# FFN1 of a layer-norm, attention and 8-bit FFN kernel: w1's blocks are turned before their trip through DRAM instead of after it

## The reference, cut to what matters

```python
def _ste_quant_rows(a):
    scale = jnp.maximum(jnp.max(jnp.abs(a), axis=-1, keepdims=True) / 127.0, 1e-08)
    return jnp.clip(jnp.round(a / scale), -127.0, 127.0) * scale

def _linear8bit(x, W, b):
    col_max = jnp.max(jnp.abs(x), axis=tuple(range(x.ndim - 1)))
    outlier = col_max > 3.0
    x_in, x_out = jnp.where(outlier, 0.0, x), jnp.where(outlier, x, 0.0)
    return _ste_quant_rows(x_in) @ _ste_quant_rows(W).T + x_out @ W.T + b

xn = _layernorm(x)                                  # x: (4, 512, 512) float32
s = attention(xn, wq, wk, wv, wo)                   # causal, 32 heads of 16, one k and v head
h = _linear8bit(xn, W1, b1)                         # W1: (2048, 512)   <- FFN1
g = silu(_linear8bit(h, W2, b2))                    # W2: (512, 2048)   <- FFN2
out = x + s * g
```

## Time and profile before

| | before |
|---|---|
| time, median of 3 runs | 804.09 us (801.3 to 804.69) |
| profiled execution, its time | 802.13 us |
| span of its instructions | 800.4 us |
| mean granted clock of TensorE | 0.981 of full speed |
| TensorE matmul busy | 756.8 us, 95% |
| TensorE weight load busy | 569.1 us, 71% |
| VectorE busy | 650.9 us, 81% |
| ScalarE busy | 395.4 us, 49% |
| GpSimd busy | 274.5 us, 34% |
| DMA packets under 512 B, of all | 71808 of 115276 |

### The profile page before, as it was taken

One profiled execution on the slowest core, in us unless ns is written; L12 is line 12 of the kernel. 1 busy time (PEld: TensorE's weight loads), 2 busy tenths in 40 slices (PEclk: granted clock), 3 DMA queues, 4 the chain that ended last, 5 costly groups with the idle time before them and its releaser, 6 DMA issues. The chain is left out here.

```text
span 800.4 us, 11979 instructions
## 1 busy us (share of the span) xinstructions
PE 756.8 (95%) x4133; PEld 569.1 (71%) x4133; DVE 650.9 (81%) x1115; ACT 395.4 (49%) x670; POOL 274.5 (34%) x349
## 2 busy tenths in 40 slices
PE   5999999999999999999998998899997999999995
PEld 4878665556776767766576876688886788888884
DVE  7988999999999899995536585686868998599957
ACT  4354167767676667777633354355453333132212
POOL 7213135555555555554622112122200000036504
PEclk9999599999999999999999999999999999999999
DMA  7421303323222223334455857646332778436982
GB/s 265 146 106 53 81 21 89 82 81 95 82 83 83 82 82 100 88 108 134 158 184 141 253 149 180 171 99 149 77 71 73 270 216 263 165 106 219 307 315 105
DMA packets 115276, 110.71 MB, mean 138 GB/s; under 512 B 71808, under 2 KB 71824, under 8 KB 113680
## 3 DMA queue, kind: packets, MB, share of 16 engines
q1 hardware_dynamic: 115216, 109.95, 46.5%
HBM read 56.43 MB, written 40.37 MB: 121 GB/s over the span
## 5 line engine op out<-in xcount | busy, mean ns | idle before, releaser
L933 DVE TENSOR_REDUCE rowmax<-ps 128x2 f32<-128x512 f32 (+3 forms) x384 | 210.4, 591 | 19.6 <-PE ps L1010 18.0
L854 ACT ACTIVATE probs<-ps 128x512 f32<-128x512 f32 (+1 forms) x352 | 174.8, 558 | 71.3 <-PE ps L1023 70.0
L1010 PE MATMUL ps<-km,stack 128*128 128x256 f32 (+3 forms) x512 | 149.7, 347 | 2.2 <-PEq L195 1.9
L1023 PE MATMUL ps<-stack,ks 128*128 128x512 f32 (+1 forms) x352 | 131.4, 383 | 2.8 <-ACT probs L854 2.7
L1010 PEld LDWEIGHTS ps<-km,stack 128*128 128x128 f32 (+1 forms) x512 | 94.2, 197 | 43.2 <-DVE rowmax L933 23.8
L836 POOL TENSOR_SCALAR_AFFINE_SELECT probs<-probs 128x512 f32<-128x512 f32 x128 | 81.0, 641 | 78.3 <-ACT probs L854 77.1
L1861 PE MATMUL ps<-big_h 128*128 128x512 f32 x256 | 99.9, 390 | 2.0 <-issue 1.6
L1863 PE MATMUL ps<-big_h,big_l 128*128 128x512 f32 x256 | 99.6, 389 | 0.0
L1862 PE MATMUL ps<-big_l,big_h 128*128 128x512 f32 x256 | 99.6, 389 | 0.0
L1036 PE MATMUL ps<-probs,vones 128*32 128x512 f32 (+3 forms) x1024 | 82.2, 439 | 0.2 <-POOL probs L836 0.2
L1023 PEld LDWEIGHTS ps<-stack,ks 128*128 128x128 f32 x352 | 66.5, 189 | 11.7 <-ACT probs L854 6.2
(11 more groups left out here) (227 smaller groups left out, 1375.5 us busy)
## 6 DMA issues: line engine op xcount, KB each, us to landing
stack<-big_h SPq DMA_DIRECT2D x128, 64.0 KB, 2.0
h_scratch<-hs SPq DMA_DIRECT2D x7, 1024.0 KB, 4.5
hload<-h_scratch SPq DMA_DIRECT2D x14, 512.0 KB, 5.1
xn_scratch<-xa SPq DMA_DIRECT2D x4, 1024.0 KB, 4.4
stack<-big_l SPq DMA_DIRECT2D x64, 64.0 KB, 2.0
xi<-xn_scratch SPq DMA_DIRECT2D x16, 256.0 KB, 2.7
xe_scratch<-xm SPq DMA_DIRECT2D x16, 256.0 KB, 2.3
w2n<-in_L_ffn_W_dram SPq DMA_DIRECT2D x4, 1024.0 KB, 6.0
```

The source lines that it names most:

```text
L854: nc.scalar.activation(probs[p][:, o:o + nh * w], ps[:, STB[n % NST], 0:nh * w], ACT.Exp).then_inc(s_exp, 1)
L933: nc.vector.tensor_reduce(dst, src, AX_X, ALU.max).then_inc(s_red, 1)
L1010: last = nc.tensor.matmul(dst, stack[u % 3][rows, hp, P * qt:P * (qt + 1)], km[rows, u // KT, p0:p0 + npar, keys], start=True, stop=True)
L1023: ins = nc.tensor.matmul(ps[:, STB[n % NST], 0:nh * w].rearrange("p (h q) -> p h q", h=nh), ks[:, u // KT, p, P * kt:P * (kt + 1)], stack[ ...
```

## The change

The block turn now comes ahead of the trip through DRAM. GpSimd's rounding of tiles 2 to 15 writes its result into w1n (no longer in place into w1t), with the inner index ordered b, k, i instead of k, b, i, in runs of 32 elements. VectorE turns the blocks from w1n into w1x. SyncE stores w1x, waits for that store, and loads it back in four DMAs of 64 KB with pieces of 512 bytes into w1t, ordered a, k, j in each partition. ScalarE's high part and GpSimd's low part read w1t in that order, in runs of 32 elements. Store and load back of tile f+2 both stand in step f, as does its turn; the load of tile f+1 at the start of step f is gone. On VectorE scale_w1(f+2) comes ahead of feature_max(f-1), in step 0 ahead of low_w1(1), and the turn waits for GpSimd's rounding and for the previous store of w1x. The load of W1's rows from tile 4 on waits for the turn that reads w1n. Tile 1 is made as before.

```diff
                 def load_w1(f):
-                    if f >= 2:
+                    if f in (2, 3):
                         sp.wait_ge(s_w1m, f - 1)
+                    if f > 3:
+                        sp.wait_ge(s_w1u, f - 3)
                     sp.dma_start(w1n[f % 2][:, :], W1[P * f:P * (f + 1), :]).then_inc(s_w1n[f % 2], 16)
...
                 def keep_w1(f):
-                    sp.wait_ge(s_w1r, f + 1)
-                    sp.dma_start(w1q_d[f % 2, :, :], w1t[f % 2][:, :]).then_inc(s_w1k[f % 2], 16)
-
-                def load_w1_blocks(f):
+                    sp.wait_ge(s_w1u, f - 1)
+                    sp.dma_start(w1q_d[f % 2, :, :], w1x[:, :]).then_inc(s_w1k[f % 2], 16)
+
+                def load_w1_turned(f):
 
                     sp.wait_ge(s_w1k[f % 2], X_LOADED + 16 * (f // 2))
-                    if f > 2:
-                        sp.wait_ge(s_w1u, f - 2)
-                    for a in range(HB):
-                        rows = w1q_d[f % 2, :, :].rearrange("(b j) (k a i) -> a j k b i", b=HB, k=KT, a=HB)[a]
-                        sp.dma_start(w1x[SQ * a:SQ * (a + 1), :].rearrange("j (k b i) -> j k b i", k=KT, b=HB),
+                    for b in range(HB):
+                        rows = w1q_d[f % 2, :, :].rearrange("(a i) (b n) -> b i a n", a=HB, b=HB)[b]
+                        sp.dma_start(w1t[f % 2][SQ * b:SQ * (b + 1), :].rearrange("i (a n) -> i a n", a=HB),
                                      rows).then_inc(s_w1x, 16)
...
                 for f in range(FT):
-                    if 2 <= f + 1 < FT:
-                        load_w1_blocks(f + 1)
                     if f + 3 < FT:
                         load_w1(f + 3)
...
                     if f + 2 < FT:
                         keep_w1(f + 2)
+                        load_w1_turned(f + 2)
...
                 def round_w1(f):
                     pool.wait_ge(s_w1m, f + 1)
-                    nc.gpsimd.tensor_tensor(w1t[f % 2][:, :], w1t[f % 2][:, :], magic_row[:, :],
-                                            ALU.subtract).then_inc(s_w1r, 1)
+                    if f == 1:
+                        nc.gpsimd.tensor_tensor(w1t[f % 2][:, :], w1t[f % 2][:, :], magic_row[:, :],
+                                                ALU.subtract).then_inc(s_w1r, 1)
+                    else:
+                        nc.gpsimd.tensor_tensor(w1n[f % 2][:, :].rearrange("p (b k i) -> p k b i", b=HB, k=KT),
+                                                w1t[f % 2][:, :].rearrange("p (k b i) -> p k b i", b=HB, k=KT),
+                                                magic_row[:, :].rearrange("p (k b i) -> p k b i", b=HB, k=KT),
+                                                ALU.subtract).then_inc(s_w1r, 1)
...
-                    nc.gpsimd.tensor_tensor(w1l[f % 2][:, :, :].rearrange("p k f -> p (k f)"), w1t[f % 2][:, :],
-                                            w1h[f % 2][:, :, :].rearrange("p k f -> p (k f)").bitcast(F32),
+                    nc.gpsimd.tensor_tensor(w1l[f % 2][:, :, :].rearrange("p k (a j) -> p k a j", a=HB),
+                                            w1t[f % 2][:, :].rearrange("p (a k j) -> p k a j", a=HB, k=KT),
+                                            w1h[f % 2][:, :, :].rearrange("p k (a j) -> p k a j", a=HB).bitcast(F32),
                                             ALU.subtract).then_inc(s_w1lo, 1)
...
                     else:
-                        act.wait_ge(s_w1u, f - 1)
+                        act.wait_ge(s_w1x, X_LOADED + 16 * HB * (f - 1))
                         act.wait_ge(s_hb, NC * (f - 1))
-                        rows = w1t[f % 2][:, :]
-                    nc.scalar.copy(w1h[f % 2][:, :, :].rearrange("p k f -> p (k f)"), rows).then_inc(s_w1hi, 1)
+                        dst = w1h[f % 2][:, :, :].rearrange("p k (a j) -> p k a j", a=HB)
+                        rows = w1t[f % 2][:, :].rearrange("p (a k j) -> p k a j", a=HB, k=KT)
+                    nc.scalar.copy(dst, rows).then_inc(s_w1hi, 1)
...
                 def turn_w1(f):
-                    dve.wait_ge(s_w1x, X_LOADED + 16 * HB * (f - 1))
-                    nc.vector.transpose(w1t[f % 2][:, :], w1x[:, :]).then_inc(s_w1u, 1)
+                    dve.wait_ge(s_w1r, f + 1)
+                    if f > 2:
+                        dve.wait_ge(s_w1k[(f - 1) % 2], X_LOADED + 16 * ((f - 1) // 2))
+                    nc.vector.transpose(w1x[:, :], w1n[f % 2][:, :]).then_inc(s_w1u, 1)
...
                     if f == 0:
                         for i in range(EARLY, NT):
                             low_x(i)
+                        scale_w1(2)
                         low_w1(1)
+                    if f and f + 2 < FT:
+                        scale_w1(f + 2)
                     if f:
                         feature_max(f - 1)
                     if f + 2 < FT:
-                        scale_w1(f + 2)
-                    if 2 <= f + 1 < FT:
-                        turn_w1(f + 1)
+                        turn_w1(f + 2)
```

More of the change, by code:

```diff
@@ L1465, in high_w1 @@
                         act.wait_ge(s_aux, n + 1)
+                        dst = w1h[f % 2][:, :, :].rearrange("p k f -> p (k f)")
                         rows = ps[:, 4 + n % 4, :]
                     else:
-                        act.wait_ge(s_w1u, f - 1)
+                        act.wait_ge(s_w1x, X_LOADED + 16 * HB * (f - 1))
                         act.wait_ge(s_hb, NC * (f - 1))
-                        rows = w1t[f % 2][:, :]
-                    nc.scalar.copy(w1h[f % 2][:, :, :].rearrange("p k f -> p (k f)"), rows).then_inc(s_w1hi, 1)
+                        dst = w1h[f % 2][:, :, :].rearrange("p k (a j) -> p k a j", a=HB)
+                        rows = w1t[f % 2][:, :].rearrange("p (a k j) -> p k a j", a=HB, k=KT)
+                    nc.scalar.copy(dst, rows).then_inc(s_w1hi, 1)
                 def high_x(i):
```

## The result

| | before | after |
|---|---|---|
| median | 803.04 us (4 runs) | 790.53 us (790.14 to 791.12, 4 runs) |
| profiled execution's span | 800.4 us | 788.4 us |
| ratio to before, 95% interval | | 0.985 (0.983 to 0.987) |
| FFN1, first matmul to start of the last | 408.11 to 603.51 | 408.15 to 591.30 |

A forecast was written before the change was run, and what follows sets the result against it. FFN1's steps 1 to 8 were held up by w1's late preparation, as idle TensorE and lower clock. Median 804.09 less 14.20, all other terms at nothing, gave 789.9 us; range of 8 in 10: 786.5 to 796.5.

The forecast's parts named there:

- The sum of 14.20 us: FFN1, steps 1 to 8: 103.80 us where eight undisturbed steps take 89.60; the change gives back all 14.20 us.
- The reading of the steps: FFN1: undisturbed steps take 11.20 us; the excess of steps 1 to 8 is idle time before steps and lower clock.
- The clock part: TensorE, steps 2 and 8: busy throughout yet 1.6 us long at granted clock 0.87; to become 1.00.
- The added wait on SyncE: SyncE stands still 2.1 to 3.1 us per step until the store lands; h's store 3.5 us late, nothing follows.
- rival 2: SyncE's new wait is passed on: w2's turns wait, VectorE some 2 us late in four steps; 798 us, chance 0.04.
- Placement: Store and load back both in step f: 3.2 us of slack before ScalarE waits, 5.9 before TensorE; returns 14.20 us.
- Length of the runs: 56 loads of 64 KB in 512 B pieces instead of 128 B: 0 to 1 us per load, in the sum nothing.
- Tile 2: Its loads' data at 430 to 431.3 against a last moment of 430.85; no stall counted, up to 0.5 us on the edge.
- VectorE, at no cost: VectorE: same instructions reordered, scale_w1 ahead of feature_max; the rounding ends inside feature_max's 2.28 us, so no cost.
- GpSimd and ScalarE in short runs, at nothing: Low and high parts in runs of 32 elements: taken as 0, since a GpSimd row with 64 B pieces was no slower.
- A wait is paid twice: TensorE in FFN1: after an idle wait the clock stood at 1.2 instead of 2.4 GHz; both payments go with it.

The follow-up runs named there:

- e6: The changed kernel with the load's pieces back at 128 bytes, turn ahead and new place kept: 800.27 us, ratio 0.999 to before.
- e3: The changed kernel with the four loads issued behind the step's w2 stores instead of ahead of them: 787.69 us, ratio 0.981 to before.
- e4: The changed kernel with the three later loads of W2's rows cut from 1 MB to 64 KB each: 788.09 us, ratio 0.982 to before.
- e9: The changed kernel with seven 1 MB stores of h's tiles cut to 64 KB, later stores filling the other 960 KB: 787.74 us, ratio 0.982 to before.
- e1: The kernel before with only the load of tile f+2 moved into step f, right behind its store: 803.86 us, ratio 1.002 to before.
- e2: The changed kernel with the load put back to its old place; turn ahead and 512-byte pieces stay: 790.92 us, ratio 0.986 to before.
- e8: The kernel before with the load of tile f+2 moved into step f, behind the step's w2 stores: 790.84 us, ratio 0.988 to before.
- e5: e2 with the load's pieces back at 128 bytes (turn ahead, load in the old place): 790.18 us, ratio 0.987 to before.
- e10: e6 with the loads moved behind the step's w2 stores, as in e3: 788.2 us, ratio 0.983 to before.
- e7: e3 with VectorE's old order, scale_w1 behind feature_max again and in step 0 behind low_w1(1): 790.62 us, ratio 0.986 to before.
- e12: e3 again with more runs, on one chip with the unaltered changed kernel: 787.90 us, ratio 0.982 to before.
- e11: The changed kernel unaltered, timed on one chip with e12: 789.08 us, ratio 0.984 to before.

## Why the prediction was right, and where it wasn't

The time: 789.9 forecast, 790.53 measured, range held. The 0.6 us between them is flattered: the gain was forecast at 14.20 us and measured at 12.5, and the median of before, with one run more, came down by 1.05. It is also luck that the time held with a wrong account of where the gain comes from. The pieces, priced at nothing, could not have been left as they were: the same kernel with 128-byte pieces gains nothing (e6). What held was the sum over the steps.

**The sum of 14.20 us.** The reading of the steps held: all five old stalls and the two steps at 0.87 of the clock are gone. What I mis-sized was that they would leave nothing behind. Steps 1 to 8 are 12.03 us shorter, not 14.20; two stalls remain, and steps 4 and 8 are 1.09 and 1.34 us over the others' 11.15. The clock part was right: 1.00 in all of them. Steps 9 to 15 gave 0.2 us that I hadn't counted (below).

**The added wait on SyncE** is the step that failed. I took 2.1 to 3.1 us from the earlier trace rows, where the four loads stood between h's store and the store of the rounded rows. In the changed kernel's crowded steps (1, 2, 3, 6 and 7) it follows h's store within about 1 us, and over the 14 stores it lands in 3.7 us in the median and in up to 10.0 (9.0 of them standing still). I had named what waits behind SyncE, but not what lies ahead of the store in the DMA queue. That was rival 2, in another form: not w2's turns waited (VectorE's wait for w2's stores is 1.6 us in all), but the loads of w1's own tiles. e3, e4 and e9 each take one element of it away, and each removes the stalls. The rival's 2 us in four steps were 1.1 and 1.3 us in two. Of h's store I wrote that nothing follows from its being late, with its buffer wanted after 28 us. The first eviction of step f+2 wants it after 25.2 (22.4 and one bank's 2.8); the store of step 2 went out after 19.2 us, and ScalarE waited for it until 28.0, 4.7 us in all, in step 4, at no cost to TensorE.

**Placement.** I wrote that the gain comes from where the trip stands. That was wrong as I meant it: the load alone, moved as the change moves it, brings nothing (e1), and put back it takes nothing away that can be told (e2). The place pays only when SyncE isn't made to stand still for it (e8: 0.988 from the place alone). What carries the gain in the old place is the turn ahead of the trip with VectorE's new order (e5: 0.987 with 128-byte pieces; the two weren't parted there): after the landing only the high and low parts are left. I had listed that as a side effect. That this shorter path is the reason is read from the order of the work; no run takes it alone.

**Length of the runs** at nothing was wrong in the changed kernel and right elsewhere: 0.2% in the old place (e2, e5), 0.2% with SyncE kept moving (e3, e10), both inside the intervals, but 1.4% in the changed kernel (e6). I had looked at the landing, where 512 B give 0.4 us (2.0 against e6's 2.4), and passed over the issue, where they give 0.86 us in each step to the engine that was about to run out of time. The page of the Trainium skill that I set against it (DMA: Bandwidth & Descriptors, Rules for kernel authors) says to wait late on a DMA's semaphore, and here that was the more valuable half of its advice: e3 does just that. The runs agree with it (0.981 against 0.985).

**Tile 2.** No stall, as in the sum: ScalarE took its high part at 428.04, straight behind bank 1, and the low part was done at 430.02, 2.7 us ahead of step 2. The four new loads were issued within 1.76 us. It is a tight tile all the same: TensorE waits for it in e1, e2, e5, e7 and e8.

**VectorE, at no cost:** its new order does no harm, but the wait that it puts first, for the raw rows of W1, is up to 6.3 us in step 8 and holds feature_max back; no row of before showed that load late in these steps, because it wasn't queued in a jam.

**GpSimd and ScalarE in short runs, at nothing:** right. The row with 64-byte pieces told it.

**A wait is paid twice:** only some are. Before, of idle stretches of 3.79, 0.92, 2.37, 0.44 and 2.54 us, two (3.79 and 2.54) were followed by a lower clock; in e8 one of 1.89 us was, and in e7 one of 1.63 us was not. So the length of the wait alone doesn't tell: 1.89 us was enough where 2.37 was not. The sum wasn't hurt by it, because it was made from whole steps, not from idle time.

## What to carry to other kernels

Before a wait for a DMA is added to the engine that issues DMAs, look at what will be in flight ahead of it at its new place, and take its landing time from rows with the same neighbours; put issues that are ready anyway between the store and the load back, which brought 0.4% here with 512-byte pieces (e3 against after) and 1.6% with 128-byte ones (e10 against e6), as much as the longer pieces or more. A queue that stands still makes its own jam, and issue time then counts (0.86 us in each step was 1.4% of the whole, e6), though the same time is free in a queue with room (e10). When four edits bring a gain together, the one whose mechanism reads best need not be the one that carries it.

## What the runs showed of the hardware

Issue time on SyncE goes with the number of pieces, and with what was issued just before: four loads of 64 KB take 1.74 us with 512-byte pieces and 2.60 us with 128-byte ones (after, e6), but 3.03 and 3.5 right behind h's 1 MB store (e2, and before at 428.19 in the earlier trace rows). A store of 256 KB lands in 2.1 us with free queues (e2's median) and in 9 us behind 2.25 MB that were issued in the 1.5 us before it (step 3 of after).

An undisturbed step of FFN1 has two lengths, 11.20 and 11.15 us, with the same 48 matmuls at the full clock. Before, e1, e4, e5 and e9 run at 11.20, after, e2, e3, e7 and e12 at 11.15; e6 has both, and e10 changes from 11.20 to 11.15 in step 4 with no stall there. It isn't tied to the length of the pieces, nor to the kernel: e11 is the changed kernel unaltered, and its steps 1 to 3 take 11.20 us where the first trace has 11.15. The cause stays open; over FFN1 it is worth 0.7 us, and it is the 0.2 us that steps 9 to 15 gave and the sum didn't hold, with some 0.4 in steps 1 to 8.
